# A graph network's edge passes: all seven loads of destination rows of a batch on SyncE, none on ScalarE

## The reference

```python
# layer 0 ("mlp")
m = maximum(concat([x[src], x[dst], edge_feats]) @ W1 + b1, 0) @ W2 + b2
out = segment_sum(m, dst, N)
# layer 1 ("gatv"), 4 heads of 16 features
xl, xr, e = x @ W_l + b_l, x @ W_r + b_r, edge_attr @ W_e
logits = einsum('ehc,hc->eh', leaky_relu(xl[src] + xr[dst] + e), att)
ex = exp(logits - segment_max(logits, dst)[dst])
out = segment_sum(xl[src] * (ex / segment_sum(ex, dst)[dst])[..., None], dst)
```

## Time and profile before

| | |
|---|---|
| median of 3 runs | 6610.97 us (6607.07 to 6613.7) |
| the profiled execution: time, span | 6620.37 us, 6618.7 us |
| first edge pass, second edge pass in the trace | about 80 to 2720 us, 2790 to 5250 us |
| busy: PE, DVE, POOL, ACT | 74%, 58%, 61%, 29% of the span |
| mean granted TensorE clock | 0.63 of full speed |

### The profile page before, as it was taken

The page is one execution under the profiler, slowest core; times in us unless marked ns, Lnnn a source line. Parts: engine busy times, 40 slices in busy tenths (PEclk is TensorE's granted clock), DMA queues, the critical chain, the costliest instruction groups (busy, mean ns, idle before and its releaser), DMA issues. The chain is left out here.

```text
span 6618.7 us, 104783 instructions
## 1 busy us (share of the span) xinstructions
PE 4926.0 (74%) x33518; PEld 3702.2 (56%) x33518; DVE 3854.6 (58%) x7688; ACT 1920.7 (29%) x4445; POOL 4014.0 (61%) x4125
## 2 busy tenths in 40 slices
PE   5566777777777776467777777777776469999689
PEld 4455666766667765356666566666655332222289
DVE  3122355555555542356666666666665469999855
ACT  1111222222222211112222222222211149999811
POOL 4555566666666665366666666666666627787634
PEclk6555566565565555555555555555555579999899
DMA  6644355555555544244444444444444334343298
GB/s 164 113 111 132 103 150 150 148 144 146 145 149 149 148 136 116 65 118 130 132 132 131 131 127 130 132 131 131 131 131 115 72 101 129 124 129 124 69 336 301
DMA packets 897045, 902.75 MB, mean 136 GB/s; under 512 B 635824, under 2 KB 779480, under 8 KB 880373
## 3 DMA queue, kind: packets, MB, share of 16 engines
q1 hardware_dynamic: 568404, 708.29, 33.9%
q0 software_dynamic: 115488, 115.45, 9.0%
q10 hardware_dynamic: 212608, 72.31, 4.8%
HBM read 656.88 MB, written 239.54 MB: 135 GB/s over the span
## 5 line engine op out<-in xcount | busy, mean ns | idle before, releaser
L507 POOL DMA_INDIRECT mlp_G<-mlp_src,src_cols x1612 | 1531.3, 950 | 1027.5 <-PE mlp_z L873 480.7
L507 POOL DMA_INDIRECT gatv_G<-gatv_src,src_cols x1612 | 1529.2, 949 | 940.1 <-DMA X<-in_x 435.7
L691 DVE TENSOR_TENSOR mlp_hots<-mlp_in_psum,src_lo 128x1024 bf16<-128x1024 bf16 x608 | 416.6, 685 | 734.3 <-remote 573.7
L909 PE MATMUL gatv_sums<-gatv_msg,gatv_same 128*128 128x68 f32 x3234 | 712.0, 390 | 151.7 <-issue 149.8
L909 PEld LDWEIGHTS gatv_sums<-gatv_msg,gatv_same 128*128 128x128 f32 x3234 | 688.2, 310 | 171.2 <-issue 169.1
L909 PE MATMUL mlp_sums<-mlp_zs,mlp_same 128*128 128x64 f32 x3234 | 676.5, 389 | 64.8 <-issue 64.6
L909 PEld LDWEIGHTS mlp_sums<-mlp_zs,mlp_same 128*128 128x128 f32 x3234 | 648.4, 301 | 66.0 <-issue 65.9
L2201 POOL TENSOR_TENSOR keys<-src_lo,gsoft_ring 128x512 f32<-128x512 f32 (+1 forms) x448 | 505.1, 1133 | 182.5 <-ACT src_lo L2344 172.7
L2266 PE MATMUL gsoft_acc<-keys,masks 128*64 128x512 f32 (+1 forms) x1568 | 558.2, 621 | 77.0 <-DVE keys L2440 42.1
L869 PE MATMUL gatv_z<-attr_w,gatv_attrT 112*128 112x448 f32 x462 | 422.3, 1017 | 206.3 <-DVE gatv_msg L597 107.9
L873 PE MATMUL mlp_z<-mlp_win,mlp_hot 128*128 128x64 bf16 x4851 | 384.6, 232 | 240.2 <-issue 236.2
(11 more groups left out here) (481 smaller groups left out, 8498.5 us busy)
## 6 DMA issues: line engine op xcount, KB each, us to landing
mean_block<-blocks SPq DMA_DIRECT2D x62, 1568.0 KB
gsoft_ring<-blocks SPq DMA_DIRECT2D x105, 896.0 KB
sums_gatv<-gatv_out_rows SPq DMA_DIRECT2D x231, 252.0 KB
mlp_rel<-rel_rows SPq DMA_DIRECT2D x116, 448.0 KB
gatv_rel<-rel_rows SPq DMA_DIRECT2D x116, 448.0 KB
sums_mlp<-mlp_out_rows SPq DMA_DIRECT2D x231, 224.0 KB
blocks<-masks SPq DMA_DIRECT2D x31, 1568.0 KB
blocks<-work SPq DMA_DIRECT2D x31, 1568.0 KB
```

Source lines behind the costliest of these rows:

```text
L507: pool.indirect_dma_start(out=G[:, b.gq, j * L.gathered:(j + 1) * L.gathered], out_offset=None, in_=L.gather_table, in_offset=bass.Indirec ...
L691: last = nc.vector.tensor_tensor(hot_of[:, slot(b, k), :, :, :], bc(steps2_of[:, 0:w, :], 1, [P, OCTET // K2, w, K2]), bc(of_step[:, cols] ...
L909: last = pe.matmul(sums[b.q % 2][:, j * L.msg:(j + 1) * L.msg], same[:, b.q, j, :], rhs, start=True, stop=True)
```

## The change

The constant SP_TILES goes. SP issues all seven window loads of a batch behind one register load, and ACT's wait for `z_made`, its register load and its three loads per batch go. The number and size of the transfers, their buffers, and the count that PE waits for on `win_in` stay. Over 462 batches 1386 loads move from ACT's queue to SP's, and 462 register loads go. In the changed kernel the line numbers from L57 on are lower by one, and those behind ACT's removed lines by five.

```diff
--- before.py
+++ after.py
@@ -54,7 +54,6 @@
 PASS_TAILS = TAIL_GROUPS[:2]
 TA = (P + 72) * B
 RA = TA // P
-SP_TILES = 4
 FIRST_CHUNKS = 1
 EARLY, EARLY_SOFT = 1, 8
 SG = 4
@@ -402,7 +401,7 @@
                             sp.dma_start(attrT[0:ax * groups[0][1], b.four, :, :, :].rearrange("r f g e -> r (f g e)"),
                                          S["attr"][ax][bass.ds(b.fours, 1), :, :].rearrange("n r e -> r (n e)")
                                          ).then_inc(attr_in[b.four], 16)
-                        load_windows(nc, sp, L, S, win, win_in, b, range(0, SP_TILES))
+                        load_windows(nc, sp, L, S, win, win_in, b, range(B))
                 o = i + (-1 - sums_after)
                 if o.exists():
                     wait(sp, sums_copied, o.used())
@@ -824,10 +823,6 @@
                         act.activation(to, build_ps[:, a * P:(a + 1) * P], ACT.Copy).then_inc(cols_copied, 1)
 
             def step(i):
-                w = i + 2
-                if L.window and w.exists():
-                    wait(act, z_made, w.used(Q))
-                    load_windows(nc, act, L, S, win, win_in, w, range(SP_TILES, B))
                 p, d = i + (-1), i + (-2)
                 if d.exists() and builds(d):
                     copy_octet(d, per_batch - 1)
```

## The result

The changed kernel takes 6637.67 us (median of 8 runs, 6619.07 to 6644.73) against 6612.34 us (8 runs). The ratio is 1.0028, with an interval of 1.0016 to 1.0041: slower by 19 us, 11 to 27. The ratio weighs all runs, whose means lie 19 us apart; the two medians lie 25 us apart. The profiled execution took 6631.66 us against 6620.37, a difference of 11.3 us.

The account below looks back on a forecast made before the run. POOL was taken to bound the kernel, its gathers and the idle time before them filling both passes. The terms 0 - 3 + 4 + 10 + 10 = +21 us on the median 6610.97 gave 6632 us, range 6590 to 6675.

Parts of the forecast that it names:

- slower by over 0.2%: Whole kernel: the case joining the forecast of 6632 us with the slower rival of 6676 us; chance 0.46.
- The steady passes, 0: Middle of both passes: three more loads per batch on SP hide in its 4.5 us wait for copied sums; 0 us.
- The rival that SP's longer streak slows the others: First-pass octet batches: more transfer issues hold up PE's completion 1.15 us in a quarter of 152 batches; 44 us, chance 0.11.
- SP's time per load: SP's window loads in steady batches: 0.85 to 0.89 us each, three more costing 2.6 us per batch.
- SP's wait falls to about 2 us per batch: SP's wait for the copied sums, expected to fall from 4.5 us to about 2 us per batch.
- The register loads, 0: ACT's go; SP's stay one per batch, seven numbers being the same instruction as four, median 1.147 us; 0 us.
- ACT's relief, -3: ACT's queue, whole kernel: 1.95 us per batch removed, useful only where its next work is ready; -3 us, at most 25.
- The start, +4: Start of each pass: the first batch's seven loads come from one queue, about 2 us per pass; +4 us, bounds 0 and 10.
- The first twenty batches, +10: 60 to 760 us: two long SP bursts grow by 5.4 and 10.0 us, of which 10 us count; bounds 0 and 25.
- The five stretches of step lists, +10: Where SP issues without a break, windows come later; 2 us for each of five stretches, +10 us in all.
- The skill's rule: Whole kernel: issuing from several engines saves only initiation time, so by this rule alone the sum would be 0.

Follow-up runs that it names:

- the two passes: Kernel before with SP issuing all seven windows in the first pass alone (5788.16 us, +18 us), or in the second alone (5754.39 us, -9 us).
- its three parts: Kernel before changed in one part alone: first-pass batches 0 to 57 (ratio 1.0043), first-pass batches 58 to 230 (0.9994), second pass (0.9984).
- second session: Follow-up runs in which the kernel before had a median of 6705.32 us; the changed kernel, timed again, took 6768.5 us, ratio 1.009.
- all but the lists: SP issues all seven windows except in batches 0 to 57 of the first pass, split 4 and 3 as before; 6750.3 us, ratio 1.0066 to the kernel before.
- third session: Follow-up runs in which the kernel before had a median of 6698.97 us; profiled again there without change, it took 6696.98 us, ratio 0.9997.
- split at 2 modulo 4: As all but the lists, but first-pass batches numbered 2 modulo 4 are also split 4 and 3; 6717.76 us, ratio 1.0032 to the kernel before.
- split at 1: As all but the lists, but first-pass batches numbered 1 modulo 4 are also split 4 and 3; 6700.57 us, ratio 1.0004 to the kernel before.
- first session: Follow-up runs in which the kernel before had a median of 5767.36 us and the change was made in single parts of the passes.
- the octets alone: Kernel before with SP issuing all seven windows in batches 58 to 230 of the first pass alone; 5765.24 us, ratio 0.9994.

## Why the prediction was right, and where its steps were not

**The total.** +21 us was forecast, +19 was measured (6632 against a median of 6637.67), and slower by over 0.2% was the likeliest case. That it came out so close is in part luck. In the pair of profiles at the first timing, batches 0 to 57 of the first pass, which were given +22 us (2, 10 and 10), end 2.7 us earlier than before, and the rest of that pass, given at 0, takes 11 us more. A single profile is uncertain by some 10 us in the former (see the stretches below), but it doesn't bear the split out. In other sessions the total differs too: +60 us was measured in the second, and the parts of the first add up to +9 (the two passes) or +12 us (its three parts).

**The steady passes, 0.** This step failed for the first pass. That the loads hide in SP's wait was right as arithmetic: 4.5 us of waiting fell by 3.5. It was wrong to conclude that nothing else moves. The prediction called itself wrong if POOL's idle time moves by more than 0.03 us per batch. In 1000 to 2000 us it went from 382.4 us in 93.3 batches to 386.7 in 92.7, by 0.07 us per batch. From batch 58 to the end the first pass took 11 us more in the profile after than in that of before, nearly all of the 11.3 us by which the profiles differ. In the second session the kernel with all but the lists took 30 and the changed one 25 us more than the kernel before in the third; the second session has no trace of the kernel before, so these two compare across sessions. For the most part these sit in cycles of 13 to 14.7 us. Within the third session, seven loads in three of four batches cost 16 us there when split at 2 modulo 4, and nothing (-2) when split at 1. The rival that SP's longer streak slows the others, given at 44 us and 1.15 us in a quarter of the batches, named the right kind of thing, with the wrong shape: 2.5 to 4 us in 7 to 18 of 135 cycles. The second pass was right within 2 us at the first timing and within 0.5 us in the third session, where both split kernels have seven loads on SP throughout it. Across the second and third it is +7, and in the first session -9.

**SP's time per load.** Taken as 0.86 us. In the cycles shown seven loads take 4.75 to 6.36 us, 0.68 to 0.91 each. The forecast that SP's wait falls to about 2 us per batch was too high: it is 1.0.

**The register loads, 0.** This term was wrong for SP, and it is part of why SP's wait fell further. It is one instruction still, but its median grew from 1.147 us for four numbers to 1.751 us for seven. It has nothing to do with held completions: in the first session it is 1.159 us for four and 1.771 us for seven, and ACT's for three takes 0.715 and 0.719 us. The 0.6 us lies where SP has idle time in a steady batch.

**ACT's relief, -3.** Not measured alone. The nearest is the second pass of the first session, where SP's loads aren't stretched and the change as a whole gains 9 us. That it is ACT's relief is not shown.

**The start, +4.** It was too large: 0.2 us at PE's first `z` and 1.6 us at the gathers of batch 4 in the first pass; the fourteen loads there take 9.79 us, 0.70 each, where 0.86 was taken.

**The first twenty batches, +10.** At batch 20 the gathers are 9.6 us later. In the second session they are 10.1 us later in the changed kernel than in that with all but the lists. The two streaks grew by 6.5 and 12.6 us, where 5.4 and 10.0 were given. This term was right with held completions. In the first session it is 0.

**The five stretches of step lists, +10.** In the first profile after, the 9.6 us of batch 20 are gone by batch 36, and batch 56 is 2.8 us earlier than before. In the second session the changed kernel is 27.4 us later at batch 56 than that with all but the lists, so by this pair the stretches add 17 us; and in the first session the run that has only batches 0 to 57 changed takes 25 us more. One profile can't tell a term of 10 us here, since two executions with the same code in batches 0 to 57 (the second pass alone changed, and the octets alone) took 540 and 551 us for them in the first session.

**The skill's rule.** The Trainium skill, page "DMA: Bandwidth & Descriptors", section "Issuing engines are not separate DMA queues", has issuing from several engines save only the time to initiate, usually small beside the transfer. By it alone the sum would have been 0. The first session agrees for the batches in which SP has idle time: seven loads take 3.43 us there, and batches 58 to 230 cost nothing. The second doesn't, with +44 us outside batches 0 to 57. In the third, where seven loads take 5 to 6 us, one kernel costs 21 us and the other, with as many loads moved, 3 us (-3 to 9).

**What stays open.** Why a completion of PE is seen up to 5 us late at the first timing and in the second and third sessions, and not in the first and fourth, is not known; neither is whether that goes by chip, since number 9 is on record for one of each, nor what part the clock has in it. That a late `rel` goes with longer cycles is shown by counts. Whether it is `rel`, the spilling windows or the store of the sums was tried once, in a session that doesn't hold completions, and is left unsettled. That the place of the streaks matters and not only their number is shown by the two split kernels.

## What to carry to other kernels

A queue whose idle time covers a longer job can still pass the delay on: ask not only whether the work fits, but what stands behind it and at which moment of the cycle that now starts. Here four batches in a row are alike but for which large transfer comes along, and the cost sat in one of the four, so count cycles one by one, by their position in the pattern, before trusting a mean of 1000 us. And a difference of 0.3% that rests on how instructions are stretched was 0.9% in the next session that timed it, so time the parts again where the whole is used, and beside a kernel before from the same session.

## What the runs showed of the hardware

The same program took 5767, 6612 and 6700 us in different sessions. Between the fastest and the others the cycle of the first pass differs by 2.0 to 2.4 us, which is about POOL's wait for `z_made`. In the fastest one SP's load instruction takes at least 0.332 us, with a median of 0.333 and a maximum of 1.732 us, where at the first timing it goes from 0.002 to 1.364 us in the changed kernel. The gathers themselves take 944 to 946 ns in both.

A register load from memory grows with the numbers that it brings, held completions or not: medians of 0.715 us for three (ACT), 1.147 us for four and 1.751 us for seven (SP) at the first timing, and 0.719, 1.159 and 1.771 us in the first session.
